# Attention scores in two rings of three accumulator banks, freed head by head, with halved context products in the last attention

## What is computed

```
x = x + 0.5 * _L0_ffn_ref(_layernorm(x, axis=-1), ...)     # mixture of 8 experts, top 1
x = x + _L0_attn_ref(_layernorm(x, axis=-1), ...)          # 16 heads, causal, relative position bias
x = x + 0.5 * _L0_ffn_ref(_layernorm(x, axis=-1), ...)
x = x + 0.5 * _L1_ffn_ref(...);  x = x + _L1_attn_ref(...);  x = x + 0.5 * _L1_ffn_ref(...)   # causal, scores A1*A2
x = x + 0.5 * _L2_ffn_ref(...);  x = x + _L2_attn_ref(...);  x = x + 0.5 * _L2_ffn_ref(...)   # a recurrence
x = x + 0.5 * _L3_ffn_ref(...);  x = x + _L3_attn_ref(...);  x = x + 0.5 * _L3_ffn_ref(...)   # full attention
```

```
scores = jnp.einsum('bhqd,bhkd->bhqk', q, k) / jnp.sqrt(jnp.asarray(HD, x.dtype))
probs = jax.nn.softmax(scores, axis=-1)
ctx = jnp.einsum('bhqk,bhkd->bhqd', probs, v)
```

## Time and profile before

| | us |
|---|---|
| median of 3 runs | 1691.52 (1687.26 to 1704.38) |
| the profiled execution, its own time | 1693.16 |
| its span, first to last instruction | 1691.5 |
| mean granted TensorE clock | 0.852 of 2.4 GHz |
| busy: PE, DVE, ACT, POOL | 1214.9, 856.0, 608.0, 501.2 |

### The profile page before, as it was taken

How to read it: one execution, slowest core, us unless ns; L and a number is a source line. 1 busy time by engine, 2 the same in 40 slices (tenths; PEclk the granted TensorE clock), 3 DMA queues, 4 the chain that set the end, 5 groups by cost and what they waited for, 6 DMA issues and landing times. The chain is left out here.

```text
span 1691.5 us, 24375 instructions
## 1 busy us (share of the span) xinstructions
PE 1214.9 (72%) x8689; PEld 695.3 (41%) x8689; DVE 856.0 (51%) x2249; ACT 608.0 (36%) x1233; POOL 501.2 (30%) x551
## 2 busy tenths in 40 slices
PE   2745899894877759999968775833923888887294
PEld 2532555552664525555535533421621122222162
DVE  5034556542135467666625496850045779981102
ACT  1211444442322135655532132310411377673131
POOL 5333112112230067665100030244433111102442
PEclk9975999997888979999989896865965599997597
DMA  9422422103511046555309000021422121200243
GB/s 205 118 67 66 101 69 65 34 18 103 148 55 33 1 118 198 172 155 169 92 18 131 0 7 0 1 66 47 131 71 65 57 64 36 78 11 12 84 120 106
DMA packets 146337, 130.83 MB, mean 77 GB/s; under 512 B 19344, under 2 KB 129828, under 8 KB 146225
## 3 DMA queue, kind: packets, MB, share of 16 engines
q1 hardware_dynamic: 128480, 108.81, 23.5%
q10 hardware_dynamic: 11088, 8.70, 2.3%
q0 software_dynamic: 6656, 11.88, 2.2%
HBM read 81.86 MB, written 48.37 MB: 77 GB/s over the span
## 5 line engine op out<-in xcount | busy, mean ns | idle before, releaser
L2011 DVE TENSOR_REDUCE att_maxima<-psum 128x2 f32<-128x1024 f32 (+3 forms) x384 | 355.6, 951 | 190.5 <-PE psum L1653 89.5
L1882 ACT ACTIVATE att_probs<-psum 128x512 f32<-128x512 f32 (+1 forms) x640 | 320.4, 553 | 275.4 <-PE psum L1692 114.9
L103 POOL TENSOR_TENSOR rstd<-var_eps,neg_half 128x4 f32<-128x4 f32 x52 | 53.4, 1027 | 635.8 <-DVE var_eps L94 635.8
L1715 PE MATMUL psum<-att_probs,att_values 128*32 128x512 f32 (+3 forms) x1536 | 171.9, 523 | 2.5 <-ACT att_context_t L1889 2.2
L739 POOL DMA_INDIRECT returned<-moe_out,moe_slot_tokens x112 | 107.9, 963 | 183.4 <-DVE moe_out L701 141.3
L1673 PE MATMUL psum<-att_queries,att_keys 50*128 50x512 bf16 (+3 forms) x512 | 123.6, 361 | 33.5 <-ACT att_probs L1882 24.1
L138 PE MATMUL psum<-ident,normalised_rows 128*128 128x128 f32 x192 | 45.4, 382 | 140.2 <-DVE normalised_rows L112 129.8
L1633 PE MATMUL psum<-att_keys,att_queries 48*128 48x512 bf16 (+3 forms) x512 | 96.3, 384 | 43.8 <-DMA att_keys<-score_terms 26.7
L638 ACT ACTIVATE moe_hidden<-psum,moe_b 128x320 f32<-128x320 f32 (+1 forms) x128 | 77.5, 607 | 134.2 <-PE psum L586 132.1
L593 PE MATMUL psum<-moe_w,moe_hidden 128*128 128x128 f32 (+1 forms) x896 | 110.3, 279 | 13.2 <-ACT moe_hidden L638 10.5
L593 PEld LDWEIGHTS psum<-moe_w,moe_hidden 128*128 128x128 f32 (+1 forms) x896 | 101.7, 184 | 22.8 <-issue 11.2
(11 more groups left out here) (244 smaller groups left out, 2139.1 us busy)
## 6 DMA issues: line engine op xcount, KB each, us to landing
score_terms<-att_parts SPq DMA_DIRECT2D x44, 384.0 KB, 2.6
moe_w<-l_w SPq DMA_DIRECT2D x64, 256.0 KB
moe_back<-returned SPq DMA_DIRECT2D x24, 256.0 KB, 4.1
att_queries<-score_terms SPq DMA_DIRECT2D x64, 96.0 KB
att_keys<-score_terms SPq DMA_DIRECT2D x64, 96.0 KB
att_queries<-score_terms SPq DMA_DIRECT2D x16, 384.0 KB, 4.1
att_keys<-score_terms SPq DMA_DIRECT2D x16, 384.0 KB, 5.6
dispatched<-untaken SPq DMA_DIRECT2D x2, 2064.0 KB, 27.3
```

What stands on the lines that cost most here:

```text
L1715: mm = nc.tensor.matmul(o_bank[VW * j:VW * (j + 1), first_query[s]:T], values[:, b % 2, s, GH * (G % GROUPS) + j, :], probs[:, G % 2, j, o ...
L1882: nc.scalar.activation(probs[:, G % 2, 2 * p + r, unit_at[u]:unit_at[u] + w], g.psum[:, cols_bank + r, 0:w], ACT.Exp).then_inc(probs_ready, 1)
L2011: ins = nc.vector.tensor_reduce(maxima[:, G % 2, t, 2 * p:2 * p + 2], g.psum[:, rows_bank(k):rows_bank(k) + 2, c0:c0 + w], axis=AX, op=ALU ...
```

## The change

1. The row pass uses a ring of three banks, 0 to 2, one bank for each head in turn, and the column pass a ring of three, 3 to 5. (Before: four and two.)
2. Row pass: the place's two heads wait together, before the first, until the maxima of all heads up to the first head of the place before are taken. PE reports each head by itself; DVE takes the maxima with one instruction per head and tile instead of one per pair and tile (768 instructions instead of 384, each half as wide) and frees each head by itself.
3. Column pass: one wait for both heads, on the exponentials of the first head of the place before. (Before: the first head waited for the same event, the second for the second head's.)
4. Last attention: `context_half` at every place 0 to 7 instead of `context_step` at 1, 3, 5, 7: the first or second 256 of the 512 columns. It waits only for the exponentials it reads, which are those of the slot before up to that unit. ACT's `copy_context` moves from behind the exponentials of place 0 to ahead of them.

```diff
-    context_at = {1: 0, 2: 1, 4: 2, 5: 3} if causal else {1: 0, 3: 1, 5: 2, 7: 3}
+    context_at = {1: 0, 2: 1, 4: 2, 5: 3} if causal else {x: x for x in range(X)}
...
-        rows_bank = lambda k: 2 * (k % 2)
-        cols_bank = 4
+        BANKS = 3
+        rows_bank = lambda k: k % BANKS
+        cols_bank = lambda k: BANKS + k % BANKS
...
             def rows_unit(G, p, u):
-                i, k = G % RING, G * X + p * U + u
-                if k >= 2:
-                    pe.wait_ge(rows_taken, k - 1)
+                i, k = G % RING, 2 * (G * X + p * U + u)
+                if k + 1 >= BANKS:
+                    pe.wait_ge(rows_taken, k + 2 - BANKS)
...
             def columns_unit(G, p, u, r):
                 i, k, j = G % RING, 2 * (G * X + p * U + u) + r, 2 * p + r
-                if k >= 2:
-                    pe.wait_ge(probs_ready, k - 1)
+                if r == 0 and k + 1 >= BANKS:
+                    pe.wait_ge(probs_ready, k + 2 - BANKS)
...
+            def context_half(G, x):
+                s, half = divmod(x, 2)
+                if half == 0:
+                    pe.wait_ge(probs_ready, 2 * (X * G + U + s + 1))
+                if x == 0:
+                    pe.wait_ge(v_ready, G // GROUPS + 1)
+                    if G >= 1:
+                        pe.wait_ge(o_copied, G)
+                for j in range(GH):
+                    mm = nc.tensor.matmul(o_bank[VW * j:VW * (j + 1), 2 * P * half:2 * P * (half + 1)],
+                                          values[:, G // GROUPS % 2, s, GH * (G % GROUPS) + j, :],
+                                          probs[:, G % 2, j, offset[s] + 2 * P * half:offset[s] + 2 * P * (half + 1)],
+                                          start=x == 0, stop=s == GROUP - 1, skip_group_check=True)
+                if x == X - 1:
+                    mm.then_inc(o_psum, 1)
...
             def row_maxima(G, x):
                 p, u = divmod(x, U)
-                k, c0 = G * X + x, 0
-                v.wait_ge(rows_psum, k + 1)
-                for t in row_units[u]:
-                    w = keys_seen[t]
-                    ins = nc.vector.tensor_reduce(maxima[:, G % 2, t, 2 * p:2 * p + 2],
-                                                  g.psum[:, rows_bank(k):rows_bank(k) + 2, c0:c0 + w], axis=AX, op=ALU.max)
-                    c0 += w
-                ins.then_inc(rows_taken, 1)
+                for r in range(2):
+                    k, c0 = 2 * (G * X + x) + r, 0
+                    v.wait_ge(rows_psum, k + 1)
+                    for t in row_units[u]:
+                        w = keys_seen[t]
+                        ins = nc.vector.tensor_reduce(maxima[:, G % 2, t, 2 * p + r:2 * p + r + 1],
+                                                      g.psum[:, rows_bank(k), c0:c0 + w], axis=AX, op=ALU.max)
+                        c0 += w
+                    ins.then_inc(rows_taken, 1)
```

More of the change, by code:

```diff
@@ L1655, in rows_bias @@
                                                       start=False, stop=chunk == 1, skip_group_check=True)
+                                if chunk == 1 and t == row_units[u][-1]:
+                                    mm.then_inc(rows_psum, 1)
                     else:
@@ L1684, in columns_bias @@
             def columns_bias(G, p, u):
-                c0, pair = 0, PAIRS * (G % GROUPS) + p
+                k, c0, pair = 2 * (G * X + p * U + u), 0, PAIRS * (G % GROUPS) + p
                 for s in units[u]:
@@ L1864, in _ @@
                         for r in range(2):
-                            columns_mask(r, u)
+                            columns_mask(n, p, u, r)
                     if x in turn_at:
@@ L1934, in split_turn @@
                 if turn == 0:
-                    if 0 <= n - 2 < NG:
+                    if kind == 0 and 0 <= n - 2 < NG:
                         copy_context(n - 2)
@@ L1989, in _ @@
                     write_untaken(g, act, (1,))
+                if kind == 3 and 0 <= n - 2 < NG:
+                    copy_context(n - 2)
                 for x in range(X):
```

29 lines of the change are left out of this document (15 added, 14 removed).

## The result

| | before | after |
|---|---|---|
| median, us | 1692.55 (1684.89 to 1710.5, 20 runs) | 1701.87 (1695.33 to 1707.02, 20 runs) |
| ratio | | 1.0044, 95% interval 1.0025 to 1.0064 |
| span of the profiled execution | 1691.5 | 1698.8 |
| mean granted clock in it | 0.852 | 0.852 |

The account below looks back on a forecast made before the run. PE was taken to bound the first two attentions, PE and DVE nearly both the last. Terms -7.0 + 4.4 (first), +15.5 + 2 (second), -8 (last) made +6.9 on 1693.2: 1700.1 profiled, 1698.5 median, range 1681 to 1714.

Parts of the forecast that it names:

- Half maxima: DVE's row maxima: one head's 512 columns take 0.69 us, starts 0.61 apart, a pair 1.22 instead of 1.13.
- The DVE rival: Halves don't overlap, 1.38 a pair, so DVE becomes the bound: +18 in the last attention, 1716 us; chance 0.17.
- First attention: Column pass there: 24 second-head waits of 0.49 removed, 11.8 us saved, 4.8 lost at place 1, net -7.0; start +4.4 apart.
- the 4.8 of late maxima at place 1: First attention, place 1: in about 6 slots PE waits some 0.8 for DVE's late maxima, 4.8 us lost.
- Second attention: Row pass there waits bare for DVE: +8.2 at place 0, +5 at place 3, +2.3 elsewhere, together +15.5; start +2 apart.
- the mean of 0.59: Second attention, place 0: the later row wait costs 0.59 us on average over 14 slots, +8.2.
- Start: Last attention's row-only slots at half clock: a place takes 1.40 instead of 1.13, +3 us in all.
- Tail: Last attention's slots 14, 15 and context only, without row pass: 35.5 falls to 25.7 us; taken as -8, bounds -4, -10.
- the walk through a slot: Last attention at full clock, place by place: 12.0, 12.6 or 15.0 a slot, 51.6 for four; -3 us for twelve.
- The row wait costs little in the second attention: Rival: PE catches up because its stalls give ACT and DVE time; +2 instead of +17.5, 1683 us; chance 0.15.
- the last falls to 1.10 a place: Rival, last attention: DVE's extras fit in PE's odd jobs, 11.0 a slot, 25 saved instead of 3, 1676 us; chance 0.10.
- The clock: Rival, last attention: longer waits at its start delay the rise from half clock, 1702 to 1710 us; chance 0.08.

Follow-up runs that it names:

- experiment 1: Only the row maxima split by head, with four row banks, two column banks and whole context steps as in the kernel before: 1.0042, 1688.6 against 1681.0 us.
- experiment 6: Changed kernel with the second head's column-bank wait put back in the first attention alone, three banks kept: 1.0112 of the kernel before.
- experiment 7: Kernel of experiment 2 with the second attention's row pass made to wait one and a half places back, as with three banks: 1.0052 of the kernel before.
- experiment 2: Changed kernel with four row banks and two column banks again in the second attention only: 0.9989 of the kernel before.
- experiment 5: Changed kernel with the row pass using all six score banks during each attention's row-only slots: 0.9973 of the kernel before.
- experiment 4: Changed kernel with four row banks and two column banks in all attentions, split maxima and context halves kept: 1.0001 of the kernel before.
- experiment 10: Kernel of experiment 8, but two-head maxima and whole context steps outside the first attention: 0.9925 of the kernel before.
- experiment 8: Changed kernel with three-bank rings in the first attention only, four and two banks elsewhere, six banks in row-only slots: 0.9909, 1668.3 against 1684.0 us.
- experiment 3: Changed kernel without context halves: whole steps at places 1, 3, 5, 7 and the copy where it was before: 1.0058 of the kernel before.
- experiment 12: Changed kernel with the last attention's odd job of place 4 moved to place 5: 1.0066 of the kernel before.
- experiment 11: Kernel of experiment 10 with the context halves in the last attention: 0.9878, 1673.3 against 1691.6 us, 6 runs.
- experiment 9: The kernel before run once more, unchanged, as a control with a second profile: 0.998 of the kernel before.

## Why the prediction was right, and where it was not

**Half maxima.** Right: 681 ns against 0.69, and 3.68 us for six (the row at 1369.40 above), so (3.68 - 0.68) / 5 = 0.60 from one to the next where I had taken 0.61. The fixed cost named in the Trainium skill ("VectorE: DVE Perf Modes", section on the TRN2 errata), about 150 cycles an instruction, would by itself have made 1.38 of a pair, an estimate; the trace does not agree for two that follow each other at once, a pair costs 1.20. The DVE rival is out, by this row and by experiment 1.

**First attention.** The mechanism was right: experiment 6 takes the gain away and gives the old slots back. The size was too small. I took 24 second-head waits of 0.49, 11.8 in all, and set against them 4.8 for place 1. The 11.8 were nearly right: the stretch from the column pass to the next work behind it takes 1.80 at 14 places 4 and 7 places 1 of before's trace, and 1.30 to 1.32 at all of these in the changed kernel; over 30 such places the sum fell from 49.9 to 39.5, by 10.4. The failed step is the 4.8 of late maxima at place 1: the row pass's new wait of 0.34 lies where ACT's first wait of 0.47 was, at place 1 too, and costs nothing in the slot that I read. In sum it costs nothing either: between two traces without the stop in slot 8, from the first copy to the last, 191.7 with the old banks (experiment 1) became 180.2 (7), -11.5, of which those stretches make some -9.4. With the wait put back it was 193.5 (6). I had -7. The slots gained unequally: 1.14 or 1.15 in slots 1, 2, 8, 10 and 11, some 0.8 in slots 3, 4, 6 and 7, and 0.25 in slot 5. The start was +4.3 for a forecast of +4.4; that close a match is luck, as starts of the same code differ: 44.4 and 46.2 before, 49.0 to 50.7 with rings (53.2 in experiment 6, which has the wait).

**Second attention.** The mechanism was right and is the best shown thing of the study (experiments 2 and 7). Of +15.5, 10.7 came in 12 slots, and 1.5 of that is a fall of the clock in slot 4 (17.91; 16.38 in experiment 7). The first slots got 0.87 longer where I had 1.1. In slot 1, with before's second profile beside it, the rows of place 4 follow 0.78 later (2.32 after those of place 3, for 1.54) and the columns 0.34 sooner after them: +0.44, my 0.4 to 0.5. From place 0 to 1 it is 2.31 for 1.98, +0.33: in this slot the mean of 0.59 was the mis-sized term, and 0.10 a slot is left for places 2, 4 and 5, or 1.4 in 14 slots of my 2.3. The row pass's idle time behind DVE is 18.8 in all, inside the 12 to 20 that I named. I had no term for the tail, which fell by 2.2: its last slot took 3.88 at full clock for 5.47 at 0.69. The start was the larger miss: +5.9 for a forecast of +2. I said that PE's own jobs hide most of the three-bank cycle; experiment 5, which has no such cycle there, gives 3.5 back, so they don't. The other 2.4 are open; starts with four banks and split maxima took 49.8, 51.1 and 52.6 (experiments 2, 1 and 4) for 49.4.

**Last attention.** The sum of -8 became +0.8. Its terms:

- Start: forecast +3. The half-clock cycle is the forecast within 0.01, rows at 1311.66, 1313.05 and 1314.44, 1.39 apart for 1.40. The mark itself moved, though: with halves the copy stands ahead of place 0. Compared between kernels with halves, 47.5 (experiment 4) and 50.4, it is +2.9, part of which is the clock (0.62 and 0.57 over the start).
- Tail: 34.1 and 30.4 for the last three slots, -3.7 for a forecast of -8. The windows of before's second profile, of the changed kernel's, and of experiment 7's, from the thirteenth copy to the last:

```profile
1510.77:1544.93 34.16, 30.64 (x159) 8.85 (x158) 6.75 (x32) 18.66 (x37) 6.32 (x6) 0.75 0.03 8
```

```profile
1526.25:1556.66 30.41, 27.08 (x261) 10.54 (x260) 7.35 (x35) 19.37 (x38) 6.33 (x6) 0.83 0.03 10
```

```profile
1520.71:1546.21 25.50, 23.28 (x261) 9.72 (x260) 7.35 (x35) 19.25 (x39) 6.37 (x6) 1.00 0.04 12
```

  At full clock the new tail takes 25.50; I had 25.7 for a stretch that begins 1.4 earlier. The old one takes 29.1 at a clock of 0.94 (experiments 1 and 10), so 3.6 is the most that the change gives. It comes from the column ring: with halves and without rings the tail takes 27.9 at full clock (experiments 4 and 8), with rings and without halves 24.6 (3). In its two slots with a column pass the halves rather cost, 20.3 against 19.4. The failed step: I set the old tail at a clock of 0.76 against a new one at full clock and took only 2 off for it, and booked the clock as a gain of the change. The new tail itself I had nearly right.
- Steady: forecast -3, measured +7.4. The step that failed is the walk through a slot. The windows of slots 4 to 6, changed kernel and then before's second profile, both at full clock:

```profile
1415.22:1457.39 42.17, 35.53 (x330) 12.69 (x328) 36.73 (x81) 28.74 (x57) 9.33 (x10) 1.00 0.21 67
```

```profile
1405.02:1444.38 39.36, 35.12 (x233) 10.73 (x232) 34.20 (x56) 28.84 (x57) 9.34 (x10) 1.00 0.22 69
```

  DVE's busy time rose by 2.5 in these three slots, as worked out (2.9 for four). Its idle time was to fall from 5.9 to 2.1 in four slots, since ACT's waits go. It didn't: 5.2 and 5.4 in three. ACT's waits went (3.6 us of idle time in the column pass of the whole attention), and waits between PE and DVE stand in their place (experiment 12). I had named slots over 13.5 as a sign of being wrong: slots 4 and 5 took 14.36 and 14.64 at full clock, for 13.76 and 12.90 before.
- Much of the rest of the +7.4 is the clock. Slot 3 in the changed kernel took 15.88 and in experiment 5, the same code there, 13.57:

```profile
1399.34:1415.22 15.88, 13.85 (x108) 4.11 (x108) 12.70 (x25) 9.51 (x19) 0.00 (x0) 0.79 0.09 27
```

```profile
1382.63:1396.20 13.57, 11.04 (x108) 3.70 (x108) 12.51 (x25) 9.51 (x19) 0.00 (x0) 1.00 0.10 31
```

  Which part of the change costs the steady part can mostly be read from one profile each, so roughly. 12 slots take 158.1 or 158.2 with pairs and whole steps (three profiles of three), 161.0 with split maxima (experiment 1), 160.4 with halves (11), 163.8 and 164.7 with both (8 and 4) and 165.0 to 166.7 with the rings too (2, 5, 6, 7, 12 and the changed kernel). On this path most of the loss is in the splitting and the halves, and little of it in the row ring, which is where I had looked. But the parts don't simply add: with split maxima and whole steps the rings bring it from 161.0 to 166.1 (3). That loss of 5.1 is not in the slots at full clock, which are the shortest of all (experiment 3); six of 12 are below full clock there, for two in experiment 1. So the halves lengthen slots at full clock and the rings go with a lower clock. I forecast the two together as a gain.

**The rivals.** "The row wait costs little in the second attention" and "the last falls to 1.10 a place" did not happen. The clock, given 0.08 as a case of its own, was not a case but a share of every term of the last attention. "DVE becomes the bound" is out in the form that I gave it (halves that don't overlap).

**The sum.** +6.9 forecast, +7.3 between the spans, and the agreement is luck in part: in these profiles the first attention came out 2.3 better than forecast, the second 3.3 better, the stretches between them 2.8 better, and the last attention 8.8 worse. Two of these hold chance of their own: the stop in slot 8, which both profiles have, and the clock. What the rows did carry is the sign of the first two attentions and of their starts, and the price of a half maximum.

## What else the runs showed

**The same wait, and behind it a fall of the clock of 6.6 us, of about 3, or none.** In slot 3 of the changed kernel's last attention the row pass waits 1.57 us, and the clock is at half right behind it (timeline, then windows of 1 us, whose last three numbers are PEclk, DMA share and GB/s):

```profile
1400.47 0.39 PE L1634 MATMUL psum<-att_keys,att_queries 48*128 48x512 bf16 x2 [1.57 <-DVE att_maxima L2034]
...
1401.04 1.08 PE L1720 MATMUL psum<-att_probs,att_values 128*32 128x256 f32 x8
...
1405.26 1.11 PE L1746 MATMUL psum<-ident,att_context_t 128*128 128x128 f32 x4
```

```profile
1400.00:1401.00 1.00, 0.53 (x4) 0.25 (x4) 0.97 (x3) 0.00 (x0) 0.00 (x0) 0.97 0.00 0
1401.00:1402.00 1.00, 1.00 (x10) 0.20 (x8) 0.93 (x4) 0.89 (x2) 0.00 (x0) 0.50 0.29 54
...
1408.00:1409.00 1.00, 1.00 (x14) 0.35 (x12) 1.00 (x2) 0.84 (x2) 0.00 (x0) 1.00 0.01 1
```

Half a context step takes 1.08 there instead of 0.64, though PE is busy 0.8 of each microsecond or more. Experiment 5 has the same wait in the same slot, and its clock stays full:

```profile
1383.77 0.39 PE L1636 MATMUL psum<-att_keys,att_queries 48*128 48x512 bf16 x2 [1.57 <-DVE att_maxima L2041]
...
1384.31 0.64 PE L1727 MATMUL psum<-att_probs,att_values 128*32 128x256 f32 x8
```

All six profiles with rings and halves have this wait of 1.57. Slot 3 then took 15.88 and 15.90 (changed kernel, experiment 6), 14.16 to 14.34 (2, 7 and 12) and 13.57 (5). So the wait alone doesn't settle it, and what does is open. A clock below full is in three or four of the 12 steady slots of these profiles, and in one of 12 in both of the kernel before.

**Time goes with the mean clock from run to run.** Within a kernel the correlation of the two lies between -0.93 (before, the 12 runs of experiment 9) and -0.48 (experiment 5); in the changed kernel's 20 runs it is -0.49. The slope is 0.9 to 1.6 us for each 0.001 in all but one (0.6 in the six runs of experiment 11). The changed kernel's median clock is 0.849 in 20 runs, that of experiment 3 0.848 in 12, of before 0.8545 in 12, of experiment 4 0.8595 in 12. At 1.1 us for each 0.001, a value from the middle, this would make some 6 us of the difference between the changed kernel and before, and most of the 7 us between experiments 1 and 4. It is a correlation, across chips in part: what lowers the clock and what lengthens the run are not told apart by it, and why halves go with a higher clock (in all three pairs that differ in them, experiments 1 and 4, 10 and 11, 3 and the changed kernel, the one with halves is faster, though the intervals overlap each time) stays open. So does the cause of the stop in slot 8.

## What to carry to other kernels

A fixed set of accumulator banks is a distance between two engines, and moving one bank from one ring to another moves slack: it pays where the reader of that ring was waited for and the bank lets that wait go (first attention, up to 1.15 a slot) and costs where the other ring had just enough (second, 0.87 a slot), so decide it loop by loop, and give all banks to the one ring that is in use at a start. When waits on one engine are removed, ask which engine pair is next and whether the extras of both can still overlap at the new distance; here they added. And before reading a term of a few us from one profile, compare the same slots in two profiles at the same granted clock.
